# Inner products of the key projection one row block earlier, and a pair's first two key features inside its query projection

## The chip, the cores and the metric

The kernel runs on one core of a Trainium2 chip. The metric is the device time of one launch in microseconds (us). The kernel before took 1494.13 us, the median of 3 runs (1493.5 to 1495.38).

## What is computed

A layer norm of x (1250 rows, 1024 columns) feeds two branches: a two-layer graph convolution, and a linear attention with 16 heads of 64 columns and 256 random features. Their sum with x goes through a second layer norm and a mixture of 8 experts with the best 2 taken per row. The change touches the attention alone:

```python
q = heads(hidden_states @ Wq)
k = heads(hidden_states @ Wk)
v = heads(hidden_states @ Wv)
q_prime = jax.nn.relu(q @ proj)
k_prime = jax.nn.relu(k @ proj)
kv = jnp.einsum('bhsf,bhsd->bhfd', k_prime, v)
attn = jnp.einsum('bhsf,bhfd->bhsd', q_prime, kv)
norm = jnp.einsum('bhsf,bhf->bhs', q_prime, k_prime.sum(axis=2))[..., None]
attn = attn / (norm + EPS)
```

## The kernel before

**Number format.** Every fp32 product is made of three passes over high and low parts (`COMBOS`): high by high, high by low, low by high. So each result that leaves PSUM and is multiplied again is read out twice: ScalarE (ACT) copies it into the high part, then VectorE (DVE) subtracts that copy from PSUM and writes the low part. Only after the second reading is the PSUM region free (an `AT` product is only copied out, by ACT, and its norm for h = 0 by DVE).

**Attention by pairs.** The 16 heads are worked as 8 pairs, p = 0 to 7. Rows come in 10 tiles of 125, and a projection has 1250 columns as three pieces of 418. A pair is this work on TensorE (PE):

- `("K", p)` and `("Q", p)`: key and query projection (`slab_product`, L1829), 8 row blocks kt = 0 to 7 of 9 matmuls each.
- `("KK", p, i)`, i = 0 to 9: key features of row tile i (L1936), 4 matmuls; the ReLU is in the read-out (ACT L1052, DVE L1421). PSUM has three banks for them.
- `("KV", p, i)`: kv sum over the tiles (L1951), 6 matmuls, into its own bank `kvb`. `("S", p)` is its transpose (L1761).
- `("QP", p, h, f)`: query features of head h, half f (`feature_product`, L1771), 6 matmuls; read out by ACT L1064 and DVE L1438.
- `("AT", p, h)`: attention product of head h (`attention_product`, L1785), 18 matmuls, which needs `S` and both `QP` of its head.
- `RC` on DVE: the reciprocal of the norm (L1452) and the product with it (L1170, `num`). `RH` splits the result (`att_h`, `att_l`), and it is stored to `at_d`.
- `E`: a group of edges of the adjacency matrix, 4 bf16 matmuls (L1663) from one-hot tiles that DVE makes (`EO`, L1174); ACT copies the sum to `stage`, and GpSimd adds it to memory by DMA.

**Work inside work.** A pair's `QP(p,0,1)`, `AT(p,0)`, `QP(p,1,0)` and `QP(p,1,1)` don't stand alone on PE: they are issued between row blocks of the next key projection `K(p+1)`, `AT(p,1)` behind block 1 of `Q(p+1)`, and the groups `E` of edges behind blocks 2, 4, 5, 6 and 7 of `K(p+1)` (`PARTS`) and block 5 of `Q(p+1)`. In `K(p+1)` the order within one kt is: row block, then group, then transpose (kt = 0), then `AT` or `QP`. In the kernel before these lie at:

```python
if kt == 0:
    kv_transposes(p)
if kt == 3:
    attention_product(("AT", p, 0))
feature = {1: ("QP", p, 0, 1), 4: ("QP", p, 1, 0), 6: ("QP", p, 1, 1)}.get(kt)
```

**PSUM.** Two regions of three banks, slot 0 and slot 1, take nearly all products; `lsb` and `kvb` are single banks. `places_of()` walks `ORDER`: an ordinary product takes the region whose turn it is, and a product listed in `INNER` takes the other one. `free_slot(k)` makes PE wait until the product that had the region before `k` (`BEFORE[k]`) has been read out. For pair p from 1 to 6 this gives: `QP(p,0,0)`, `QP(p,0,1)`, `AT(p,0)`, `QP(p,1,0)`, `QP(p,1,1)` and then `Q(p+1)` follow one another in slot 0, each waiting for the one before; `K(p+1)`, then `AT(p,1)`, then the key features `KK(p+1, ...)` follow one another in slot 1.

**Order of the engines.** The list `ORDER` from `steps()` is the order in which every engine takes its own part of each step, and the semaphore counts come from positions in it. ACT and DVE work strictly in that order. Around the change, DVE's order in `K(p+1)` is `EO`, low part of a slab (`P`), `S`, `EO`, `QP(p,0,1)`, `EO`, `VL` (low part of the values), `AT(p,0)`, `EO`, `QP(p,1,0)`, `EO`, `QP(p,1,1)`, `K(p+1)`, `P`, `EO`, `EO`, `RC(p)`, then `KK(p+1,0)`, `KK(p+1,1)` and `KK(p+1,2)`. ACT's has `QP(p,0,1)`, `E`, `VL`, `AT(p,0)`, `E`, `QP(p,1,0)`, `E`, `QP(p,1,1)`, `E`, `K(p+1)`.

**The last pair** has no next projection to hide in. Its steps run one behind the other (p = 7), and two things are bound to DMA there: `AT(7,0)` is read out into tiles that the stores of pair 6 must have left (`att_stored`), and SyncE (SP) has begun to load the stored pairs back for the output projection, the first three of them when `Q(7)` is complete (`load_att`, L675). GpSimd's queue writes two blank tiles of 1680 KB in the same stretch, behind the last group of edges.

Of the kernel before, what the change touches and what calls it, by code (L numbers as in the profile page):

```python
# [28 lines left out]
T = 125  # L29
# [3 lines left out]
KD = D // 128  # L33
# [73 lines left out]
def steps():  # L107
# [30 lines left out]
    o += [("EO", q0[1]), ("VL", 0), ("P", 2)] + [("EO", g) for g in q0[2:]] + [("E", g) for g in q0] + [("Q", 0)]  # L138
    for p in range(PAIRS):
        more = p + 1 < PAIRS  # L140
        o += [("KK", p, 0), ("KK", p, 1), ("KK", p, 2)]
        if p:
            last = WITHIN[("Q", p)][1]
            o += [("EP", last), ("E", last)]
        for i in range(3, NT):
            o += [("KV", p, i - 3), ("KK", p, i)] + {4: [("QE", p, 0)], 7: [("QE", p, 1)]}.get(i, [])
        if not more:
            o += [("KV", p, NT - 3), ("KV", p, NT - 2), ("RH", p - 1), ("QP", p, 0, 0), ("KV", p, NT - 1), ("KC", p),
                  ("QP", p, 0, 1), ("S", p)]
            o += [("QP", p, 1, 0), ("QP", p, 1, 1), ("AT", p, 0), ("AT", p, 1), ("RC", p), ("RH", p)]  # L150
            continue
        o += [("KV", p, NT - 3)] + ([("RH", p - 1)] if p else [])
        o += [("QP", p, 0, 0), ("KV", p, NT - 2), ("KV", p, NT - 1), ("KC", p)]
        g, (q0, q1) = WITHIN[("K", p + 1)], WITHIN[("Q", p + 1)]
        n = SLAB[("K", p + 1)] + 1
        o += [("EO", g[0]), ("P", n), ("S", p), ("EO", g[1]), ("QP", p, 0, 1), ("E", g[0]), ("EO", g[2]), ("VL", p + 1),
              ("AT", p, 0), ("E", g[1]), ("EO", g[3]), ("QP", p, 1, 0), ("E", g[2]), ("EO", g[4]), ("QP", p, 1, 1),
              ("E", g[3]), ("K", p + 1), ("E", g[4])]
        o += [("P", n + 1)] if n + 1 < len(SLABS) else []
        o += [("EO", q0), ("AT", p, 1), ("EO", q1), ("E", q0), ("Q", p + 1), ("RC", p)]  # L160
    for f in range(KD):
        if f == KD - 1:
            o += [("DT",), ("ZP", 1, 0)]
# [47 lines left out]
ORDER = steps()  # L211
INNER = {("XT", i) for i in range(1, NT)} | {("AT", p, 1) for p in range(PAIRS - 1)}
INNER |= {("FT", i) for i in range(NT - 1)}
INNER |= {k for p in range(PAIRS - 1) for k in (("S", p), ("QP", p, 0, 1), ("AT", p, 0), ("QP", p, 1, 0), ("QP", p, 1, 1))}
OTHER = INNER | {("QP", p, 0, 0) for p in range(PAIRS - 1)}
AMID = {(6, 3): ("RT", 0), (7, 3): ("PX", 0), (8, 1): ("RT", 1), (8, 6): ("PX", 1)}
# [17 lines left out]
def places_of():  # L234

    place, before, last, turn = {}, {}, {}, 0
    for k in ORDER:
        if k[0] not in PSUM_KINDS:
            continue
        if k[0] == "KK":  # L240
            place[k] = turn
            before[k] = last.get(turn) if k[2] == 0 else before[("KK", k[1], 0)] if k[2] < 3 else ("KK", k[1], k[2] - 3)
            last[turn] = k
            continue
        if k[0] == "OT" or k in OTHER:
            place[k] = 1 - turn
        elif k[0] in ("R", "RT"):
            place[k] = 2 + (k[0] == "RT")
        elif k[0] == "PX":
            place[k] = 3  # L250
        else:
            place[k] = turn
            turn = 1 - turn
        before[k] = last.get(place[k])
        last[place[k]] = k
    return place, before
# [43 lines left out]
def build(nc, x, src_cols, dst_cols, dst_groups, slabs, wv, w1, w2, wr, proj, feat_rows, consts, turns, tie,  # L300
          iota, keys, eye, pe, blank, before, list_blank, tokens, expert_at, b2_rows, out):
    ctx = ExitStack()
    with ctx:
# [298 lines left out]
        def kk_bank(k):  # L602

            return slot[SLOT[k]][:T, 512 * (k[2] % 3):512 * (k[2] % 3) + 2 * FEAT]
# [1028 lines left out]
        def _(ten):  # L1633
# [120 lines left out]
            def kv_transposes(p):  # L1754
# [6 lines left out]
                    mm = ten.transpose(lsb[:, 128 * q:128 * q + 128], kvt[:, 128 * q:128 * q + 128], ident[:, :])  # L1761
                mm.then_inc(s_full, 1)

            def feature_product(k, ps):

                p, h, f = k[1:]
                if h == 0 and f == 0:
                    ten.wait_ge(dve_done, DVED[("QE", p, 0)])
                for c, part in enumerate((proj_h, proj_l[h])):
                    for q in range(3):  # L1770
                        mm = ten.matmul(ps[:, 512 * q:512 * q + CW], part[:, 128 * f:128 * f + 128],  # L1771
                                        q_s[h][:, CW * q:CW * q + CW], start=(c == 0), stop=(c == 1))
                mm.then_inc(psum_full, 1)
# [40 lines left out]
            def slab_product(k, ps):  # L1814
# [5 lines left out]
                for kt in range(KD):  # L1820
                    if k == ("O", 0) and kt < KD - 1:
                        ten.wait_ge(at_landed[kt], 32)
                    if k == ("O", 0) and kt == KD - 1:
                        ten.wait_ge(dve_done, DVED[("RH", PAIRS - 1)])
                    if k == ("H", 1, 0) and kt == KD - 1:
                        ten.wait_ge(dve_done, DVED[("Z", 1, KD - 1)])
                    for c, (a, b) in enumerate(COMBOS):
                        for q in range(3):
                            mm = ten.matmul(ps[:, 512 * q:512 * q + CW], w[a][:, kt, :],  # L1829
                                            big[b][:, kt, CW * q:CW * q + CW],  # L1830
                                            start=(kt == 0 and c == 0), stop=(kt == KD - 1 and c == 2))
                    if kt == 2 and k[0] == "O" and k[1]:
                        mix_transposes(k[1] - 1)
                    if kt == 1 and k[0] == "Q" and k[1]:
                        attention_product(("AT", k[1] - 1, 1))
                    if kt == KD - 1:
                        mm.then_inc(psum_full, 1)
                    for g, part in zip(inside, PARTS[len(inside)]):
                        if part == kt:
                            if k[0] == "K" and k[1] and g == inside[0]:  # L1840
                                ten.wait_ge(dve_done, DVED[("S", k[1] - 1)])
                            group_product(g)
                    if k[0] == "K" and k[1]:
                        p = k[1] - 1
                        if kt == 0:
                            kv_transposes(p)
                        if kt == 3:
                            attention_product(("AT", p, 0))
                        feature = {1: ("QP", p, 0, 1), 4: ("QP", p, 1, 0), 6: ("QP", p, 1, 1)}.get(kt)
                        if feature:  # L1850
                            free_slot(feature)
                            feature_product(feature, sums[SLOT[feature]])

            for k in ORDER:
# [74 lines left out]
                elif kind == "KK":  # L1929

                    p, i = k[1], k[2]
                    if i == 0:
                        ten.wait_ge(dve_done, DVED[("K", p)])
                    for h in range(2):
                        for c, part in enumerate((proj_h, proj_l[h])):
                            mm = ten.matmul(kk_bank(k)[:, FEAT * h:FEAT * h + FEAT], k_s[h][:, T * i:T * i + T], part[:, :],  # L1936
                                            start=(h == 0 and c == 0), stop=(c == 1), skip_group_check=True)
                elif kind == "KV":


# [215 lines left out]
```

## Time and profile before

| | us |
|---|---|
| median of 3 runs | 1494.13 |
| the profiled execution | 1493.13 |
| its span, first to last instruction | 1491.5 |
| PE busy | 1415.6 (95%) |
| DVE busy | 852.9 (57%) |
| ACT busy | 535.4 (36%) |

The profile is of one execution. Its engine rows name the source line, the operation and the tiles (out<-in). PE matmuls are pipelined: a matmul's time reaches into the next one's, so distances between two starts are what a step costs. A row with x3 is three matmuls, and its start is that of the first. "[0.68 <-DVE qp_l L1438]" means that the engine had sat idle for 0.68 us and that the wait was ended by that work of DVE. The pairs of heads fill the stretch from about 178 to 604 us, and pairs 1 to 7 repeat with a period of 56.2 us.

### The profile page before, as it was taken

How to read it: one execution, taken by the hardware profiler on the slowest of the kernel's cores; microseconds unless marked ns; L12 is line 12 of the kernel's file. 1: busy time of each engine (PE TensorE's matmuls, PEld its weight loads, DVE VectorE, ACT ScalarE, POOL GpSimd, SP SyncE). 2: the span in 40 equal slices, each digit the busy share in tenths (PEclk: the TensorE clock that was granted, in tenths of full speed). 3: DMA queues.
4: the chain of work that ended last, by engine and by line, in shares of the span. 5: the costliest groups of instructions: out<-in, count | busy, mean ns of one | idle time of the engine just before them, and what ended most of it. 6: DMA issues, size and time to landing. Idle time of an engine off the chain costs nothing.

```text
span 1491.5 us, 20042 instructions
## 1 busy us (share of the span) xinstructions
PE 1415.6 (95%) x7718; PEld 1308.4 (88%) x7718; DVE 852.9 (57%) x1563; ACT 535.4 (36%) x621; POOL 184.9 (12%) x182
## 2 busy tenths in 40 slices
PE   6999899999999999999999999999999759999995
PEld 5788899999999998899999999999788658888884
DVE  7564678778778778622766233354667734433340
ACT  4333254354354354232122133322112235444441
POOL 0012210100110111000000000000001442223311
PEclk9999999999999999999999999999999869999998
DMA  9765433243233336686342033221565587877863
GB/s 310 237 157 122 78 52 78 46 83 74 50 80 74 54 80 214 229 199 166 97 125 70 29 98 103 81 77 46 165 177 146 176 218 188 221 205 181 199 151 77
DMA packets 97187, 194.34 MB, mean 130 GB/s; under 512 B 31715, under 2 KB 62426, under 8 KB 95373
## 3 DMA queue, kind: packets, MB, share of 16 engines
q1 hardware_dynamic: 76324, 145.83, 33.3%
q0 software_dynamic: 20768, 47.22, 17.4%
q8 instruction: 62, 1.02, 0.3%
q14 instruction: 33, 0.27, 0.1%
HBM read 129.78 MB, written 73.13 MB: 136 GB/s over the span
## 4 chain that ended last, share of the span: by engine, by line
PE 72%; DMA 14%; DVE 6%; ACT 3%; issue 2%; SPq 1%; POOL 0%; POOLq 0%; ACTq 0%; DVEq 0%
PE slot L1829 24%; PE slot L1911 12%; DMA adj_d<-stage 8%; PE slot L2057 7%; PE slot L2025 6%; PE slot L1987 5%; PE slot L1785 3%; PE kvb L2057 3%; PE kvb L1951 3%; PE slot L1771 2%; DMA adj_d<-eye_dram 2%; PE slot L2040 2%; DMA mix_d<-mixn 1%; PE slot L1936 1%; DMA dx<-x_dram 1%
## 5 line engine op out<-in xcount | busy, mean ns | idle before, releaser
L1829 PE MATMUL slot<-big_hi,slab_h 128*128 128x418 f32 x768 | 194.7, 361 | 10.8 <-DVE qp_l L1438 4.8
L1829 PE MATMUL slot<-big_lo,slab_h 128*128 128x418 f32 x768 | 189.3, 355 | 0.0
L1829 PE MATMUL slot<-big_hi,slab_l 128*128 128x418 f32 x768 | 188.2, 353 | 0.0
L1829 PEld LDWEIGHTS slot<-big_hi,slab_h 128*128 128x128 f32 x768 | 140.4, 190 | 16.6 <-DVE qp_l L1438 6.4
L1829 PEld LDWEIGHTS slot<-big_hi,slab_l 128*128 128x128 f32 x768 | 145.2, 189 | 2.3
L1829 PEld LDWEIGHTS slot<-big_lo,slab_h 128*128 128x128 f32 x768 | 145.1, 189 | 2.2
L839 POOL DMA_DIRECT2D adj_d<-stage x80 | 66.7, 834 | 484.8 <-ACT stage L919 372.3
L1911 PE MATMUL slot<-adj,xs_h 125*128 125x418 f32 x480 | 118.2, 354 | 0.8 <-DVE ztmp L1170 0.5
L1911 PE MATMUL slot<-adj,xs_l 125*128 125x418 f32 x480 | 117.4, 352 | 0.0
L1174 DVE TENSOR_SCALAR oh_src<-lane,src_lo 125x125 bf16<-125x125 f16 x320 | 84.6, 265 | 25.7 <-PE kvb L1663 18.0
L864 POOL DMA_INDIRECT list_d<-rec,spots x20 | 27.9, 1397 | 529.7 <-issue 512.4
L1911 PEld LDWEIGHTS slot<-adj,xs_h 125*128 125x128 f32 x480 | 90.4, 189 | 2.2 <-DVE ztmp L1170 0.7
L1911 PEld LDWEIGHTS slot<-adj,xs_l 125*128 125x128 f32 x480 | 90.5, 189 | 1.2
L1174 DVE TENSOR_SCALAR oh_key<-key_iota,key_rel 125x240 bf16<-125x240 int16 x320 | 90.7, 283 | 0.0
L1170 DVE TENSOR_TENSOR ws_l<-ws_raw,ws_h 128x1024 fp32r<-128x1024 f32 x32 | 38.9, 1219 | 85.6 <-ACT ws_h L919 85.6
L1170 DVE TENSOR_TENSOR slab_l<-slab_raw,slab_h 128x1024 fp32r<-128x1024 f32 x34 | 41.6, 1223 | 57.8 <-ACT slab_h L919 57.6
L899 POOL DMA_INDIRECT out_dram<-y,lists x32 | 49.1, 1533 | 181.3 <-ACT y L919 175.6
L1452 DVE RECIPROCAL nrm<-nrm 128x1254 f32<-128x1254 f32 x8 | 63.9, 7993 | 9.6 <-ACT nrm L919 9.6
L2057 PE MATMUL slot<-xe_h,ws_h 128*128 128x420 f32 x176 | 64.6, 367 | 2.2 <-DVE xe_l L1170 2.2
L1421 DVE SCALAR_TENSOR_TENSOR kk_l<-slot,kk_h 125x512 fp32r<-125x512 f32 x80 | 51.6, 686 | 26.0 <-ACT kk_h L1052 25.5
L1052 ACT ACTIVATE kk_h<-slot 125x512 fp32r<-125x512 f32 x80 | 46.0, 597 | 50.8 <-PE slot L1936 50.4
L2057 PE MATMUL slot<-xe_l,ws_h 128*128 128x420 f32 x176 | 63.2, 359 | 0.0
(316 smaller groups left out, 2940.9 us busy)
## 6 DMA issues: line engine op xcount, KB each, us to landing
slab_raw<-slabs_dram SPq DMA_DIRECT2D x40, 512.0 KB, 4.2
ws_raw<-w_dram SPq DMA_DIRECT2D x36, 512.0 KB, 7.3
adj_d<-stage POOLq DMA_DIRECT2D x81, 117.2 KB, 3.1
w_raw<-w_dram SPq DMA_DIRECT2D x9, 1024.0 KB
adj_d<-eye_dram POOLq DMA_DIRECT2D x1, 6250.0 KB, 24.8
raw<-adj_d SPq DMA_DIRECT2D x3, 1828.8 KB
dx<-x_dram SPq DMA_DIRECT2D x10, 448.0 KB
xn_d<-dx SPq DMA_DIRECT2D x10, 448.0 KB
```

The source lines that it names most:

```text
L839: pool.dma_start(adj_d[:, bass.ds(first, SPAN), :].rearrange("p d j -> p (d j)"), stage[g % 3][:, :], accum_op=ALU.add).then_inc(e_added, 16)
L899: pool.indirect_dma_start(out, bass.IndirectOffsetOnAxis(ap=lists[:, e, i, 0:1].bitcast(U32), axis=0), y[i][:, :], None, compute_op=ALU.ad ...
L1052: act.activation(kk_p[k[2] % 3][0][:, :], kk_bank(k), ACT.Relu).then_inc(act_done, 1)
L1170: return dve.tensor_tensor(o, a, b, op)
L1174: dve.tensor_scalar(o, a, s1, None, op0)
L1421: dve.scalar_tensor_tensor(out=kk_p[k[2] % 3][1][:, :], in0=kk_bank(k), scalar=0.0, in1=kk_p[k[2] % 3][0][:, :].bitcast(F32), op0=ALU.max, ...
L1452: link(dve.reciprocal(nrm[:, :], nrm[:, :]))
L1829: mm = ten.matmul(ps[:, 512 * q:512 * q + CW], w[a][:, kt, :], big[b][:, kt, CW * q:CW * q + CW], start=(kt == 0 and c == 0), stop=(kt == ...
L1911: mm = ten.matmul(ps[:, 512 * q:512 * q + CW], xs_p[t % 2][a][:, j, :], adj[:, j, CW * q:CW * q + CW], start=(j == 0 and a == 0), stop=(j ...
L1987: mm = ten.matmul(ps[:T, 512 * q:512 * q + 512], big[b][:, kt, T * i:T * i + T], rows_p[kt][a][:, 512 * q:512 * q + 512], start=(kt == 0 a ...
L2025: mm = ten.matmul(to[:RT_, 512 * q:512 * q + 512], a_p[a][:, f, RT_ * i:RT_ * i + RT_], w2_p[e % 2][b][:, f, 512 * q:512 * q + 512], start ...
L2057: mm = ten.matmul(ps, w[a][:, kt, :], xe[b][:, kt, :], start=(kt == 0 and c == 0), stop=(kt == KD - 1 and c == 2))
```

## The change

Three of the four inner products in `K(p+1)` are issued one row block earlier: `QP(p,0,1)` behind block 0 and not 1, `AT(p,0)` behind 2 and not 3, `QP(p,1,1)` behind 5 and not 6. `QP(p,1,0)` stays behind block 4. For pairs 1 to 7, `KK(p,0)` and `KK(p,1)` are issued inside `Q(p)`, behind its row blocks 5 and 6, and not behind it; `KK(p,2)` and the rest stay. They become `INNER`, so that they keep the slot that they had (1), and on every engine's list they stand behind `RC(p-1)`, as they did, and ahead of `Q(p)`. No instruction is added or removed.

```diff
@@ steps()
-        o += [("KK", p, 0), ("KK", p, 1), ("KK", p, 2)]
+        o += [] if p else [("KK", p, 0), ("KK", p, 1)]
+        o.append(("KK", p, 2))
...
-        o += [("EO", q0), ("AT", p, 1), ("EO", q1), ("E", q0), ("Q", p + 1), ("RC", p)]
+        o += [("EO", q0), ("AT", p, 1), ("EO", q1), ("E", q0), ("RC", p), ("KK", p + 1, 0),
+              ("KK", p + 1, 1), ("Q", p + 1)]
@@
+INNER |= {("KK", p, i) for p in range(1, PAIRS) for i in range(2)}
@@ places_of()
-            place[k] = turn
-            before[k] = last.get(turn) if k[2] == 0 else before[("KK", k[1], 0)] if k[2] < 3 else ("KK", k[1], k[2] - 3)
-            last[turn] = k
+            place[k] = 1 - turn if k in INNER else turn
+            before[k] = (last.get(place[k]) if k[2] == 0 else before[("KK", k[1], 0)] if k[2] < 3
+                         else ("KK", k[1], k[2] - 3))
+            last[place[k]] = k
@@ TensorE
+            def key_features(k):
+
+                p, i = k[1:]
+                if i == 0:
+                    ten.wait_ge(dve_done, DVED[("K", p)])
+                for h in range(2):
+                    for c, part in enumerate((proj_h, proj_l[h])):
+                        mm = ten.matmul(kk_bank(k)[:, FEAT * h:FEAT * h + FEAT], k_s[h][:, T * i:T * i + T], part[:, :],
+                                        start=(h == 0 and c == 0), stop=(c == 1), skip_group_check=True)
+                mm.then_inc(psum_full, 1)
@@ slab_product(k, ps)
                     if kt == 1 and k[0] == "Q" and k[1]:
                         attention_product(("AT", k[1] - 1, 1))
+                    if k[0] == "Q" and k[1] and KD - 3 <= kt < KD - 1:
+                        free_slot(("KK", k[1], kt - KD + 3))
+                        key_features(("KK", k[1], kt - KD + 3))
@@
-                        if kt == 3:
+                        if kt == 2:
                             attention_product(("AT", p, 0))
-                        feature = {1: ("QP", p, 0, 1), 4: ("QP", p, 1, 0), 6: ("QP", p, 1, 1)}.get(kt)
+                        feature = {0: ("QP", p, 0, 1), 4: ("QP", p, 1, 0), 5: ("QP", p, 1, 1)}.get(kt)
```

The walk of `ORDER` on TensorE calls `key_features(k)` for the other key features, in place of the same loop written there.

## Rows read from the trace of the kernel before

**Rows 1.** Stretches: length, busy (count) of PE, PEld, DVE, ACT, POOL, PEclk, DMA, GB/s.

```profile
175.00:197.00 22.00, 18.01 (x125) 17.52 (x126) 11.97 (x27) 9.91 (x16) 3.31 (x4) 0.92 0.29 44
253.00:309.00 56.00, 54.83 (x336) 53.25 (x335) 44.83 (x83) 26.67 (x34) 5.80 (x7) 1.00 0.35 69
```

**Rows 2.** Waits of PE in 175 to 606 us: total, times, longest.

```profile
PE kvb L1951 <- DVE kk_l L1421: 6.4, 10, 2.7
PE slot L1829 <- DVE qp_l L1438: 4.8, 7, 0.7
```

**Rows 3.** Timeline of PE (start, length), K(2): block 1, group, block 3, AT(1,0).

```profile
255.00 0.82 PE L1829 MATMUL slot<-big_hi,slab_h 128*128 128x418 f32 x3
...
259.68 0.57 PE L1663 MATMUL lsb<-oh_key,oh_src 125*125 125x240 bf16 x4
260.02 0.82 PE L1829 MATMUL slot<-big_hi,slab_h 128*128 128x418 f32 x3
...
261.83 0.73 PE L1785 MATMUL slot<-qp_h,s_h 128*128 128x418 f32 x3
```

**Rows 4.** Timeline of DVE, same stretch: QP(1,0,0), first one-hot, QP(1,0,1).

```profile
252.99 1.46 DVE L1438 SCALAR_TENSOR_TENSOR qp_l<-slot,qp_h 128x1254 fp32r<-128x1254 f32 x1
254.36 0.25 DVE L1174 TENSOR_SCALAR oh_src<-lane,src_lo 125x125 bf16<-125x125 f16 x1
...
259.41 1.46 DVE L1438 SCALAR_TENSOR_TENSOR qp_l<-slot,qp_h 128x1254 fp32r<-128x1254 f32 x1 [0.40 <-ACT qp_h L1064]
```

**Rows 5.** Timeline of PE, rear of K(2): QP(1,1,0), QP(1,1,1), last group, Q(2).

```profile
267.35 0.82 PE L1771 MATMUL slot<-qT,proj_h 128*128 128x418 f32 x3
...
272.76 0.82 PE L1771 MATMUL slot<-qT,proj_h 128*128 128x418 f32 x3
...
275.70 0.57 PE L1663 MATMUL lsb<-oh_key,oh_src 125*125 125x240 bf16 x4
276.96 0.84 PE L1829 MATMUL slot<-big_hi,slab_h 128*128 128x418 f32 x3 [0.68 <-DVE qp_l L1438]
```

**Rows 6.** Timeline of ACT, same stretch: QP(1,1,1), then both copies of K(2).

```profile
274.19 1.22 ACT L1064 ACTIVATE qp_h<-slot 128x1254 fp32r<-128x1254 f32 x1 [2.92 <-PE slot L1771]
...
275.90 2.45 ACT L919 ACTIVATE kT<-slot 64x1254 fp32r<-64x1254 f32 x2 [0.24 <-PE slot L1829]
```

**Rows 7.** Timeline of DVE, same stretch: QP(1,1,1), then both low parts of K(2).

```profile
275.44 1.46 DVE L1438 SCALAR_TENSOR_TENSOR qp_l<-slot,qp_h 128x1254 fp32r<-128x1254 f32 x1 [2.52 <-ACT qp_h L1064]
277.14 2.94 DVE L1170 TENSOR_TENSOR kT<-slot,kT 64x1254 fp32r<-64x1254 f32 x2 [0.24 <-ACT kT L919]
```

**Rows 8.** Timeline of PE: AT(1,1); key features, group, KV(2,0); KV(2,5).

```profile
280.51 0.73 PE L1785 MATMUL slot<-qp_h,s_h 128*128 128x418 f32 x3
...
294.65 0.28 PE L1936 MATMUL slot<-proj_h,kT 128*125 128x256 f32 x1
...
296.07 0.57 PE L1663 MATMUL lsb<-oh_key,oh_src 125*125 125x240 bf16 x4
296.70 0.39 PE L1951 MATMUL kvb<-kk_h,v_h 125*128 125x256 f32 x1
...
303.34 0.39 PE L1951 MATMUL kvb<-kk_h,v_h 125*128 125x256 f32 x1 [0.43 <-DVE kk_l L1421]
```

**Rows 9.** Timeline of DVE: end of RC(1), key features 0 to 2 of pair 2.

```profile
293.42 1.47 DVE L1170 TENSOR_TENSOR num<-num,nrm 128x1254 f32<-128x1254 f32 x1
295.95 1.89 DVE L1421 SCALAR_TENSOR_TENSOR kk_l<-slot,kk_h 125x512 fp32r<-125x512 f32 x3 [1.07 <-ACT kk_h L1052]
```

**Rows 10.** Timeline of SP, last pair: first load at the end of Q(7), store.

```profile
575.98 0.33 SPq L675 DMA_DIRECT2D big_hi<-at_d  x1
...
590.79 2.38 SPq L756 DMA_DIRECT2D at_d<-att_l  x1
```

**Rows 11.** Timeline of ACT, last pair: AT(7,0), released by the store.

```profile
604.25 1.21 ACT L919 ACTIVATE num<-slot 64x1254 f32<-64x1254 f32 x1 [6.58 <-DMA at_d<-att_l]
```

**Rows 12.** Timeline of PE: first block of the output projection.

```profile
605.81 0.81 PE L1829 MATMUL slot<-big_hi,slab_h 128*128 128x418 f32 x3 [1.32 <-ACT num L919]
```

More of the change, by code:

```diff
@@ L1931, in _ @@
                     p, i = k[1], k[2]
[L1932 to L1937, printed above, removed]
+                    key_features(k)
+                    continue
                 elif kind == "KV":
```

## The prediction

> **What bounds the kernel now.** I read the stretches first: in one period of a pair (253 to 309 us) PE is busy for 54.83 of 56 us at the full granted clock, DVE for 44.83 and ACT for 26.67 [rows 1]. So PE sets the pace, and since the change neither adds nor removes an instruction, it can move the time only through what PE waits for. The list of PE's waits comes next: the read-out of query features ends 7 waits with 4.8 us in all, the read-out of key features 10 waits with 6.4 us, of which 2.7 us in one, in pair 0, which the change leaves alone [rows 2]. Then I walked one period on the timelines, engine by engine, to see where PE stands against the time at which it could have gone on. The reader is to see three places there.
>
> *At the start of Q(2).* QP(1,1,1) starts at 272.76 and Q(2) at 276.96 [rows 5]. Q(2) takes the slot that QP(1,1,1) had, so it waits for ACT (274.19 to 275.41) and DVE (275.44 to 276.90), which follow each other without a gap [rows 6, 7]. From start of the product to the release of its slot that is **4.20 us**. Unhindered, Q(2) would follow the last group, which begins at 275.70 and takes 0.34 us (259.68 to 260.02 for another group), so at 276.04 [rows 3, 5]. PE loses **0.92 us**.
>
> *At KV(2,0).* The group ahead of it starts at 296.07, so KV could start at 296.41; it starts at 296.70, when key feature 0 has been read out [rows 8]. **0.29 us** lost. The page hides this one, as the group's modelled end covers it.
>
> *At KV(2,5)*: idle for 0.43 us [rows 8], the read-out of a key feature stands behind that of the query projection. Nothing in the change moves these three against each other, and I leave it at nothing.
>
> **The front of K(p+1): QP(p,0,1) and AT(p,0) earlier.** What lies between 255.00 and the group at 259.68 is the same work in another order, and the group still ends at 260.02, so AT(1,0) could start at 260.02, where block 3 stands today, and not at 261.83 [rows 3]. It needs the slot of QP(1,0,1), and so DVE. QP(1,0,1) itself can start at 255.00: the slot of QP(1,0,0) is released when DVE ends at 254.45 [rows 3, 4]. But DVE then has one-hots, slab, transpose and again one-hots in front of QP(1,0,1), from 254.36 without a gap; today it waits for only 0.40 us between them and the read-out at 259.41 [rows 4]. So the read-out of a product that comes 1.8 us earlier can move forward by only 0.40 us, or 0.48, as DVE's next instruction starts 0.09 us before the end of the one ahead (254.36 against 252.99 + 1.46) [rows 4]. I take 0.48: 258.93 + 1.46 = 260.39, and PE follows 0.06 us later (276.90 to 276.96) [rows 5, 7], at 260.45. A **new wait of 0.43 us** (0.51 at the other bound). The one who waits is PE with everything behind it.
>
> **The rear of K(p+1): QP(p,1,1) earlier.** Its position moves from behind block 6 to behind block 5, and QP(1,1,0) stays, at 267.35 [rows 5], now 0.43 later. Between the two there is left one product, one block and one group, the same work as between QP(1,1,1) and Q(2) today: 275.70 - 272.76 + 0.34 = 3.28 us [rows 3, 5]. But QP(1,1,1) needs the slot that QP(1,1,0) had, 4.20 us after its start by the chain above. A **new wait of 0.92 us**: it is the very wait that is taken away from Q(2), at another place. In exchange Q(2) finds its slot free: block 6, group, block 7 and group now lie between. **0.92 us removed.**
>
> **What that does to AT(p,1).** It is not in the diff, but it takes the slot of K(p+1). ACT starts to copy K(2) at 275.90 and DVE ends at 277.14 + 2.94 = 280.08 [rows 6, 7]; with 0.06 to PE that is 4.24 us after the copy begins. Today AT(1,1) starts 4.61 us after it, at 280.51 [rows 6, 8], and part of that distance is the wait at Q(2). With this gone the distance is 4.61 - 0.92 = 3.69 us, and PE waits for **0.55 us**. The copies can't begin earlier, K(2) is complete only just before the last group, and ACT is idle ahead of them (0.24 us) [rows 6].
>
> **The key features inside Q(p).** KK(p,0) and KK(p,1) need slot 1 after AT(p-1,1): four row blocks lie between, and ACT's two copies of K took 2.45 us [rows 6], so no wait. They cost PE what they did: three of them fill 294.65 to 296.07, 0.47 us each [rows 8]; a change of neighbour moves the time of three matmuls by up to 0.09 us (0.82 behind a group, 0.73 elsewhere [rows 3]), so between -0.09 and +0.09 us I take nothing. DVE stands in RC until 293.42 + 1.47 = 294.89 and idles for 1.07 us before the three low parts from 295.95, 1.89 us [rows 9]. With all that is ahead 1.0 us later, RC ends at about 295.9 and the low part of KK(2,0) at 296.6, while KV(2,0) is due at about 297.4: the **0.29 us is removed**, and RC in front of the key features on DVE costs nothing, with 0.8 us to spare.
>
> **The sum for a pair.** Removed: 0.92 + 0.29 = 1.21 us. New: 0.43 + 0.92 + 0.55 = 1.90 us. Net +0.69 us, and seven transitions (K(1) to K(7)) make **+4.8 us**. I take K(1) as equal to the others.
>
> **The last pair.** There PE is not the bound. AT(7,0) is copied out at 604.25, after 6.58 us of waiting for a store of pair 6 that SP began at 590.79 [rows 10, 11], and the output projection stood still for 1.32 us behind that copy [rows 12]. The store shares the DMA engines with loads that SP issues from the end of Q(7) on, at 575.98 [rows 10], and with GpSimd's blank tiles. The change brings the end of Q(7) nearer to the store: KV(7,0) comes 296.70 - 294.65 = 2.05 us after the end of Q now [rows 8], and then one key feature and one group after it, 0.47 + 0.34, so 1.24 us of distance are gone. If the DMA engines are the limit all the way from the end of Q(7), these 1.24 us are paid in full, if the store's own time counts, not at all. The blank tiles start with the last group, which comes nearer too. Between 0 and 1.2 I take the middle, **+0.6 us**.
>
> Together +5.4 us. The profiled execution took 1493.13 us, of which 1491.5 are the span; it is 1.0 us under the median of 1494.13, so I add to either: about 1498.5 us in an execution like the profiled one, and **1499.5 us** as the median.
>
> **The rivals.** *The moved waits fall under other work* (faster). Then only the removed ones count, 7 x 1.21 = 8.5 us, 1485.7 us. For it speaks that the waits in question are real and regular, seven of each. Against it that the slot's release is a chain of ACT and DVE without slack in it [rows 6, 7]; it could come true only if QP(1,1,1) did not need the slot of QP(1,1,0). *The wait only changes its place* (no difference). If AT(p,1) finds its slot free after all, the sum of a pair is 1.21 against 1.35, 7 x 0.14 = 1.0 us, with the last pair 1495.7. It decides at 0.37 us: so much slack AT(1,1) has today (280.51 against 280.08 + 0.06) [rows 7, 8]. *The clock gives way under more waits* (slower still). In 175 to 197 us, with the wait of 2.7 us in it [rows 2], the granted clock has a mean of 0.92 [rows 1]: 0.08 x 22 / 0.5 = 3.5 us at 1.2 GHz instead of 2.4, or 1.8 us lost. Once for a pair that is 12 us more, 1512 us. Against it: the period with waits of 0.68 and 0.43 us in it shows 1.00 [rows 1, 5, 8], and the new ones are under 1 us. The Trainium skill (TensorE: Matmul & The Clock Gate, A second HAM failure mode: psum-queue depth-cycling) speaks for this rival: TensorE that is idle for a moment between groups of matmuls, cycling through PSUM banks, may see its clock fall and rise again. By that rule this rival would be likely; the trace doesn't show it in the pairs. *The change doesn't do what it says*: the same instructions in a different order can't be left out, and I give it no chance of its own.
>
> **How the numbers follow.** My forecast gets 0.80; its own range is 1497.2 to 1501.5 (a pair at 0.69 - 0.25 or + 0.2, which is the bounds above, 0.08 and 0.09, and about as much again for what modelled ends hide; the last pair at 0 or 1.2). No difference gets 0.10, the faster rival 0.08, the clock 0.02. The range 1495.0 to 1502.5 holds the first and the larger part of the second. A difference of 0.2%, 3.0 us, is about what a measurement of this kernel can tell from none; the lower part of my own range is near to it, so slower by more gets 0.78, within it 0.14, faster 0.08.
>
> **What the profile after would show.** PE idle ahead of QP(p,1,1) (L1771) and AT (L1785) seven times each, released by DVE's `qp_l`, and ahead of AT(p,1) released by `kT`; no wait of L1829 for `qp_l` at Q, and no gap before KV(p,0). The period of a pair grows from 56.2 to about 56.9 us. I am wrong if AT(p,1) doesn't wait for `kT`, if DVE's `qp_l` of QP(p,0,1) comes more than 0.5 us earlier against the start of K(p+1), or if the period gets shorter.

## The result

The changed kernel takes 1500.82 us (median of 5 runs, 1500.29 to 1501.87) against 1494.13 us: 6.7 us, or 0.45%, **slower** (ratio 1.0045, 95% interval 1.0033 to 1.0056). Run again on another occasion, on one chip with the last two experiments, it gave 1.0042 (1.0029 to 1.0055). The profiled execution took 1501.87 us, with a span of 1500.2; it is the slowest of the five, so spans differ by more (8.7 us) than medians do; a table in the part on the prediction says where. In the experiments a difference in us is worked out from the ratio, and the ratio compares with the kernel before as it ran on the same occasion (medians of 1493.1 to 1494.9 us). The medians themselves can lie up to 2 us further apart.

TensorE's waits over the pairs, as in [rows 2] (engine, line and tile, who ended the wait: total us, times, longest). Lines have moved: L1844 is the row block of a projection, L1786 an inner product of the features, L1800 the attention product, L1775 the key features, L1965 the kv sum.

```profile
PE kvb L1965 <- DVE kk_l L1425: 6.5, 10, 2.7
PE slot L1786 <- DVE qp_l L1442: 5.6, 9, 0.7
PE slot L1800 <- DVE kT L1174: 2.8, 7, 0.4
PE slot L1800 <- DVE qp_l L1442: 1.9, 7, 0.3
```

The reader is to see that the seven waits of a projection for `qp_l` [rows 2] have gone, and that waits at three other places have come. Seven of the nine at L1786 are those of QP(p,1,1); two, of 0.36 and 0.46 us, belong to the last pair, as before. Seven waits of AT(p,1) are for `kT`, and seven of AT(p,0) are for `qp_l`. The timeline of PE in K(2) and Q(2) (start, length of the merged matmuls) answers [rows 3, 5, 8]:

```profile
259.77 0.57 PE L1667 MATMUL lsb<-oh_key,oh_src 125*125 125x240 bf16 x4
260.64 0.82 PE L1800 MATMUL slot<-qp_h,s_h 128*128 128x418 f32 x3 [0.29 <-DVE qp_l L1442]
...
267.93 0.82 PE L1786 MATMUL slot<-qT,proj_h 128*128 128x418 f32 x3
...
272.13 0.84 PE L1786 MATMUL slot<-qT,proj_h 128*128 128x418 f32 x3 [0.69 <-DVE qp_l L1442]
...
277.55 0.82 PE L1844 MATMUL slot<-big_hi,slab_h 128*128 128x418 f32 x3
...
281.65 0.83 PE L1800 MATMUL slot<-qp_h,s_h 128*128 128x418 f32 x3 [0.41 <-DVE kT L1174]
...
297.35 0.57 PE L1667 MATMUL lsb<-oh_key,oh_src 125*125 125x240 bf16 x4
297.69 0.37 PE L1965 MATMUL kvb<-kk_h,v_h 125*128 125x256 f32 x1
...
304.31 0.39 PE L1965 MATMUL kvb<-kk_h,v_h 125*128 125x256 f32 x1 [0.43 <-DVE kk_l L1425]
```

| wait in front of | before | forecast | after, from the rows |
|---|---|---|---|
| AT(p,0) | 0 | 0.43 | 260.64 - (259.77 + 0.34) = 0.53 |
| QP(p,1,1) | 0 | 0.92 | 272.13 - (267.93 + 3.28) = 0.92 |
| Q(p+1) | 0.92 | 0 | 0, it starts at 277.55 without a wait |
| AT(p,1) | 0 | 0.55 | 281.65 - (277.55 + 3.53) = 0.57 |
| KV(p+1,0) | 0.29 | 0 | 297.69 - (297.35 + 0.34) = 0 |
| sum | 1.21 | 1.90 | 2.02 |

Here 3.28 us is one inner product, one block and one group [rows 3, 5], and 3.53 us lies between the starts of Q(2) and AT(1,1) when nothing waits: 3.55 by [rows 5, 8], less 0.02 that a start out of a wait costs there. From KV(2,5) at 304.31 to the same place of pair 7, at 589.66, are 285.35 us, a period of 57.07; before, from 303.34 [rows 8] to 584.47, it was 56.23. Seven times 0.84 us are 5.9 us.

The last pair, as in [rows 10 to 12]: SP's queue, then ACT, then PE.

```profile
582.43 0.33 SPq L679 DMA_DIRECT2D big_hi<-at_d  x1
...
595.98 2.34 SPq L760 DMA_DIRECT2D at_d<-att_l  x1
```

```profile
611.34 1.21 ACT L923 ACTIVATE num<-slot 64x1254 f32<-64x1254 f32 x1 [8.48 <-DMA at_d<-att_l]
...
613.80 1.21 ACT L923 ACTIVATE num<-slot 64x1254 f32<-64x1254 f32 x1
```

```profile
612.90 1.39 PE L1844 MATMUL slot<-big_hi,slab_h 128*128 128x418 f32 x3 [3.22 <-ACT num L923]
```

The output projection waits 3.22 us for the copy of AT(7,0), and not 1.32. The store of pair 6 landed 15.26 us after it was issued, 13.36 before.

### The profile page after: what moved, and what is told of

Its sections match the earlier page's. It is cut to its first block, busy times and chain, and to the rows that moved or that the text cites. A ratio compares the mean times of both kernels' runs of the same rounds, so it can differ in the third digit from the quotient of the medians.

```text
span 1500.2 us, 20042 instructions
## 1 busy us (share of the span) xinstructions
PE 1418.2 (95%) x7718; PEld 1310.1 (87%) x7718; DVE 853.8 (57%) x1563; ACT 537.1 (36%) x621; POOL 184.9 (12%) x182
## 4 chain that ended last, share of the span: by engine, by line
PE 67%; DMA 14%; DVE 11%; ACT 4%; issue 2%; SPq 1%; POOL 0%; POOLq 0%; ACTq 0%; DVEq 0%
PE slot L1844 20%; PE slot L1929 12%; DMA adj_d<-stage 8%; PE slot L2071 7%; PE slot L2039 6%; PE slot L2001 5%; PE slot L1800 3%; PE kvb L2071 3%; DVE qp_l L1442 2%; PE kvb L1965 2%; PE slot L1775 2%; DMA adj_d<-eye_dram 2%; PE slot L2054 1%; DMA mix_d<-mixn 1%; DVE kT L1174 1%
## 5 line engine op out<-in xcount | busy, mean ns | idle before, releaser
L1844 PE MATMUL slot<-big_hi,slab_h 128*128 128x418 f32 x768 | 194.0, 361 | 7.8 <-ACT num L923 3.2
L1844 PE MATMUL slot<-big_lo,slab_h 128*128 128x418 f32 x768 | 190.2, 356 | 0.0
L1844 PE MATMUL slot<-big_hi,slab_l 128*128 128x418 f32 x768 | 189.1, 354 | 0.0
L1844 PEld LDWEIGHTS slot<-big_hi,slab_h 128*128 128x128 f32 x768 | 141.9, 191 | 11.4 <-ACT num L923 3.5
L1844 PEld LDWEIGHTS slot<-big_hi,slab_l 128*128 128x128 f32 x768 | 146.2, 190 | 2.4
L1844 PEld LDWEIGHTS slot<-big_lo,slab_h 128*128 128x128 f32 x768 | 145.9, 190 | 2.0
L868 POOL DMA_INDIRECT list_d<-rec,spots x20 | 27.9, 1397 | 530.3 <-issue 512.9
```

## The experiments

Theory: a PSUM slot is released 4.20 us after the start of an inner product, DVE works in the order of its list, and RC starts with AT(p,1); so each product that is moved nearer to the one ahead of it in its slot takes the wait with it, and the products behind it, which had lived on that wait, begin to wait too. The last pair is bound by DMA from the end of Q(7) on. Rival: the key features inside the query projection are what costs, and the longer store is chance.

**The inner products alone** (the kernel before, with the three new places).

```diff
-                        if kt == 3:
+                        if kt == 2:
                             attention_product(("AT", p, 0))
-                        feature = {1: ("QP", p, 0, 1), 4: ("QP", p, 1, 0), 6: ("QP", p, 1, 1)}.get(kt)
+                        feature = {0: ("QP", p, 0, 1), 4: ("QP", p, 1, 0), 5: ("QP", p, 1, 1)}.get(kt)
```

> The inner products of the key projection one row block earlier, alone; the key features stay behind the query projection, as before. Theory (waits for PSUM slots only move, and one more appears): per transition the new waits at AT(p,0), QP(p,1,1) and AT(p,1) measured in the changed kernel, 0.53 + 0.92 + 0.57 us, against 0.92 us removed at Q, net +1.10 us, seven times: 7.7 us slower than before (7 to 8.5), and the store of pair 6 in the last pair lands 13 to 14 us after its issue, as before. Rival (the key features inside the query projection are what costs, by breaking up its stream of matmuls): under 4 us slower than before.

Measured: 1503.41 us, ratio 1.0047 (1.0031 to 1.0064), 7.0 us slower; the medians are 8.5 us apart. Its waits in 195 to 575 us, which hold the key projections of pairs 1 to 7, and so seven of each:

```profile
PE slot L1771 <- DVE qp_l L1438: 4.8, 7, 0.7
PE slot L1785 <- DVE kT L1170: 2.8, 7, 0.4
...
PE slot L1785 <- DVE qp_l L1438: 2.0, 7, 0.3
```

All three new waits are there without the key features. From KV(2,5) at 299.81 to KV(7,5) at 586.64 the period is 57.37 us, 1.14 above the kernel before; 1.10 was expected. So the loss is of the inner products, and the rival is out.

**The key features alone** (the changed kernel, with the inner products back at blocks 1, 3, 4 and 6).

```diff
-                        if kt == 2:
+                        if kt == 3:
                             attention_product(("AT", p, 0))
-                        feature = {0: ("QP", p, 0, 1), 4: ("QP", p, 1, 0), 5: ("QP", p, 1, 1)}.get(kt)
+                        feature = {1: ("QP", p, 0, 1), 4: ("QP", p, 1, 0), 6: ("QP", p, 1, 1)}.get(kt)
```

> The first two key features of pairs 1 to 7 inside the query projection, alone; the inner products stay where they were. Theory: 0.29 us less in front of KV(p,0), seven times 2.0 us less up to the last pair, and there 1.2 to 1.9 us given back at the store, which then takes about 15 us to land instead of 13.4: in all between -0.9 and 0 us against before. Rival (key features inside cost something of their own): slower than before by over 1 us, and the period of a pair not shorter than 56.24 us.

Measured: ratio 0.9994 (0.9980 to 1.0008), no difference that can be told. The period is read from two rows of PE's timeline five pairs apart, the first matmuls of KV(2,5) and KV(7,5):

```profile
306.38 0.39 PE L1965 MATMUL kvb<-kk_h,v_h 125*128 125x256 f32 x1 [0.43 <-DVE kk_l L1425]
```

```profile
586.07 0.39 PE L1965 MATMUL kvb<-kk_h,v_h 125*128 125x256 f32 x1 [0.43 <-DVE kk_l L1425]
```

(586.07 - 306.38) / 5 = 55.94 us, 0.29 less than before: the gain in the pairs is the wait that was removed, and a key feature between two blocks costs nothing of its own that the period shows. Over seven pairs that is 2.0 us; the runs don't show them.

**The key features inside, but not in pair 7** (the kernel with the key features alone). The edit leaves `("KK", 7, 0)` and `("KK", 7, 1)` behind `Q(7)`; of its diff one place is shown, and `steps()` and `INNER` are changed to match.

```diff
-                    if k[0] == "Q" and k[1] and KD - 3 <= kt < KD - 1:
+                    if k[0] == "Q" and 0 < k[1] < PAIRS - 1 and KD - 3 <= kt < KD - 1:
```

> As the run with the key features alone, but pair 7 keeps its first two behind its query projection, so that the distance from the end of Q(7) to the store of pair 6 is as before. Theory (the last pair is bound by DMA from the end of Q(7) on): six times 0.29 us less, 1.7 us faster than before, the store lands 13.4 us after its issue, and this kernel is 0.8 to 1.7 us faster than the one with the key features inside Q(7) as well. Rival (the longer store was chance): the store takes the same time in both, and this kernel is 0.3 us slower than that one.

Measured: ratio 0.9993 (0.9980 to 1.0005), the same as with pair 7. The store took 14.32 us and not 13.4, so neither theory's number came out, and the runs can't tell 1 us. What bears on it is the distance of the first load of the last pair from the landing of the store, in all the profiles that still have the blank tiles there:

| kernel | first load | store issued | landed after | load to landing |
|---|---|---|---|---|
| before | 575.98 | 590.79 | 13.36 | 28.2 |
| inner products alone | 578.15 | 592.95 | 13.52 | 28.3 |
| last product alone | 578.25 | 593.06 | 13.78 | 28.6 |
| attention later | 592.47 | 606.94 | 13.54 | 28.0 |
| keys, not pair 7 | 573.95 | 588.75 | 14.32 | 29.1 |
| changed | 582.43 | 595.98 | 15.26 | 28.8 |
| changed, again | 583.83 | 597.38 | 14.31 | 27.9 |
| keys alone | 578.84 | 592.38 | 15.20 | 28.7 |
| one-hots behind | 578.35 | 591.89 | 14.63 | 28.2 |

The upper five issue the store 14.5 to 14.8 us after the first load, the lower four 13.5 us after it. The last column has a mean of 28.4 us in both, with 0.4 us of scatter from profile to profile. So, over this range, the landing follows the end of Q(7) and not the issue of the store, and the 1.24 us by which the store came nearer are given back, as far as nine profiles with that scatter can tell.

**The last product alone** (the kernel before, QP(p,1,1) behind block 5).

```diff
-                        feature = {1: ("QP", p, 0, 1), 4: ("QP", p, 1, 0), 6: ("QP", p, 1, 1)}.get(kt)
+                        feature = {1: ("QP", p, 0, 1), 4: ("QP", p, 1, 0), 5: ("QP", p, 1, 1)}.get(kt)
```

> Only the last inner product, QP(p,1,1), from behind row block 6 to behind row block 5. Theory: a wait of 0.92 us in front of it, none in front of Q, and 0.57 us in front of AT(p,1) for the read-out of K: seven times 0.57, 4.0 us slower than before. Rival (the wait only changes its place, and AT(p,1) waits in the changed kernel because of the other two moves): within 0.5 us of before, and AT(p,1) does not wait.

Measured: 1499.60 us, ratio 1.0029 (1.0018 to 1.0040), 4.3 us slower.

```profile
PE slot L1771 <- DVE qp_l L1438: 4.8, 7, 0.7
PE slot L1785 <- DVE kT L1170: 2.8, 7, 0.4
```

4.8 us of waits in seven stand now at the inner product (L1771), the same sum as at the projection before [rows 2], and AT(p,1) waits for K's low part, without the other two moves. The period is (586.75 - 302.41) / 5 = 56.87 us, 0.64 more than before. This one edit is about two thirds of the loss.

**The attention product one block later** (the changed kernel with AT(p,1) behind block 2 of the query projection).

```diff
-                    if kt == 1 and k[0] == "Q" and k[1]:
+                    if kt == 2 and k[0] == "Q" and k[1]:
                         attention_product(("AT", k[1] - 1, 1))
```

> The changed kernel with AT(p,1) behind row block 2 of the query projection and not behind block 1. Theory (AT(p,1) waits for the read-out of K, and RC on DVE starts with AT(p,1)): no wait of AT(p,1) for kT, 0.57 us less, but AT(p,1) then starts 1.15 us later than in the changed kernel, RC ends as much later, and KV(p,0) waits about 0.9 us for key feature 0, which it did not in the changed kernel: 0.3 to 0.4 us more per transition, 2 to 3 us slower than the changed kernel, 9 to 10 us slower than before. Rival (the wait at AT(p,1) comes from something else, as the S of its pair): the wait stays after the move.

Measured: 1504.61 us, ratio 1.0061 (1.0043 to 1.0080), 9.1 us slower than before.

```profile
PE kvb L1965 <- DVE kk_l L1425: 7.2, 13, 0.7
PE slot L1786 <- DVE qp_l L1442: 4.8, 7, 0.7
PE slot L1800 <- DVE qp_l L1442: 1.9, 7, 0.3
```

No wait for `kT` is left, and the kv sum waits 13 times and not 6 in 195 to 575 us. Six are new, of 0.69 us each, at KV(p,0) behind RC (a seventh, of pair 7, comes at 594.00); the seventh of the others is that of pair 0, which lies inside the window here. The period is 57.36 us, from 256.50 to 600.64 in six, 0.29 more than in the changed kernel. So AT(p,1) is held between the read-out of K ahead of it and the reciprocal behind it, and moving it one block does not win.

**DVE's one-hots behind the read-out** (the changed kernel, one entry of the order).

```diff
-        o += [("EO", g[0]), ("P", n), ("S", p), ("EO", g[1]), ("QP", p, 0, 1), ("E", g[0]), ("EO", g[2]), ("VL", p + 1),
+        o += [("EO", g[0]), ("P", n), ("S", p), ("QP", p, 0, 1), ("EO", g[1]), ("E", g[0]), ("EO", g[2]), ("VL", p + 1),
```

> The changed kernel with DVE's second set of one-hots behind its read-out of QP(p,0,1) and not ahead of it. Theory (the wait of AT(p,0) is DVE's queue): the read-out starts when ACT is done, 1.3 us earlier, AT(p,0) does not wait, and each transition is 0.53 us shorter: 3.7 us faster than the changed kernel, 3 us slower than before. The one-hots are then made 1.4 us later, far ahead of their group. Rival (AT(p,0) waits for the transpose S or for ACT): no difference to the changed kernel.

Measured: 1497.04 us, ratio 1.0015 (1.0001 to 1.0029), 2.2 us slower than before.

```profile
PE slot L1786 <- DVE qp_l L1442: 4.8, 7, 0.7
PE slot L1800 <- DVE kT L1174: 2.8, 7, 0.4
PE kvb L1965 <- DVE kk_l L1425: 2.6, 6, 0.4
```

The wait of AT(p,0) for `qp_l` is gone and the other two are untouched. The period is (585.58 - 302.74) / 5 = 56.57 us, 0.50 less than in the changed kernel. The wait came from what stood ahead in DVE's order.

**The blank tiles early** (the changed kernel; GpSimd writes them in pairs 3 and 4).

```diff
+                if g == WITHIN[("K", 4)][0]:
+                    pool.dma_start(flat_d[N:N + CAP, :], blank).then_inc(blanks_in, 16)
+                if g == WITHIN[("K", 5)][0]:
+                    pool.dma_start(out[N:N + CAP, :], blank).then_inc(blanks_in, 16)
                 first = pool.value_load(base_i[0:1, g:g + 1], min_val=0, max_val=N - 1)
...
-            pool.dma_start(flat_d[N:N + CAP, :], blank).then_inc(blanks_in, 16)
-            pool.dma_start(out[N:N + CAP, :], blank).then_inc(blanks_in, 16)
```

> The changed kernel with GpSimd's two blank tiles (3.4 MB) written during pairs 3 and 4, where the DMA engines are a third busy, and not in the last pair. Theory (the store of pair 6 shares the DMA engines with loads and blank tiles): it lands 5 to 8 us after its issue instead of 15, AT(7,0) is copied out without a wait, and the first block of the output projection starts about 3 us sooner: 2.5 to 3.5 us faster than the changed kernel. Rival (the store waits for something else, as its turn on SP's queue): it still takes over 12 us.

Measured: 1498.60 us, ratio 1.0035 (1.0021 to 1.0048) against before; the changed kernel's was 1.0045, and the intervals overlap, so the runs alone don't show a gain. The trace shows it more sharply. The store was issued at 594.87 and landed 5.5 us later, and not 15.26, as the theory had it (5 to 8 us); the rival, its turn on SP's queue, is out. ACT copied AT(7,0) out as soon as PE had made it:

```profile
605.19 1.21 ACT L925 ACTIVATE num<-slot 64x1254 f32<-64x1254 f32 x1 [3.42 <-PE slot L1802]
...
609.88 1.22 ACT L925 ACTIVATE num<-slot 64x1254 f32<-64x1254 f32 x1
```

From KV(7,5) at 588.57 that is 16.6 us; in the changed kernel it was 611.34 - 589.66 = 21.7, before 604.25 - 584.47 = 19.8 [rows 11]. The last copy, of AT(7,1), has to wait for PE then. It ends the chain that RC starts from, and comes 609.88 - 588.57 = 21.3 us after KV(7,5), where it was 613.80 - 589.66 = 24.1 in the changed kernel and 614.26 - 591.07 = 23.2 in its second profile: 1.9 to 2.8 us less.

**The best order** puts the lessons together: a distance of two blocks between QP(p,1,0) and QP(p,1,1), the one-hots and the values' parts behind the read-outs that PE waits for, and the edge group of the query projection ahead of AT(p,1), with its one-hots in DVE's idle time before K's low part. The blank tiles are early too, by the edit of the experiment before, which is not printed again.

```diff
-        o += [("EO", g[0]), ("P", n), ("S", p), ("EO", g[1]), ("QP", p, 0, 1), ("E", g[0]), ("EO", g[2]), ("VL", p + 1),
-              ("AT", p, 0), ("E", g[1]), ("EO", g[3]), ("QP", p, 1, 0), ("E", g[2]), ("EO", g[4]), ("QP", p, 1, 1),
-              ("E", g[3]), ("K", p + 1), ("E", g[4])]
+        o += [("EO", g[0]), ("P", n), ("S", p), ("QP", p, 0, 1), ("EO", g[1]), ("E", g[0]), ("EO", g[2]), ("AT", p, 0),
+              ("VL", p + 1), ("QP", p, 1, 0), ("E", g[1]), ("EO", g[3]), ("E", g[2]), ("EO", g[4]), ("QP", p, 1, 1),
+              ("E", g[3]), ("EO", q0), ("K", p + 1), ("E", g[4])]
         o += [("P", n + 1)] if n + 1 < len(SLABS) else []
-        o += [("EO", q0), ("AT", p, 1), ("EO", q1), ("E", q0), ("RC", p), ("KK", p + 1, 0),
-              ("KK", p + 1, 1), ("Q", p + 1)]
+        o += [("E", q0), ("AT", p, 1), ("EO", q1)]
+        o += [("RC", p), ("KK", p + 1, 0), ("KK", p + 1, 1), ("Q", p + 1)]
...
                     if kt == 1 and k[0] == "Q" and k[1]:
+                        group_product(inside[0])
                         attention_product(("AT", k[1] - 1, 1))
...
-                        if part == kt:
+                        if part == kt and not (k[0] == "Q" and k[1]):
...
-                        feature = {0: ("QP", p, 0, 1), 4: ("QP", p, 1, 0), 5: ("QP", p, 1, 1)}.get(kt)
+                        feature = {0: ("QP", p, 0, 1), 3: ("QP", p, 1, 0), 5: ("QP", p, 1, 1)}.get(kt)
```

> A version meant to leave out the waits that the theory names: on top of the changed kernel, one-hots behind the read-out of QP(p,0,1), the values' parts behind AT(p,0), QP(p,1,0) behind row block 3 (so that two blocks lie between it and QP(p,1,1)), the group of edges of the query projection ahead of AT(p,1) with its one-hots made before the read-out of K, and the blank tiles early. Theory: no wait for QP(p,1,1) and AT(p,0), about 0.3 us at AT(p,1), none at Q and KV(p,0): a period of about 55.3 us instead of 56.2, 6 to 7 us less over the pairs and 2 to 3 us less in the last one, 8 to 10 us faster than before. Rival: a further queue shows up, and the period stays above 56 us.

Measured: 1485.26 us, ratio 0.9937 (0.9917 to 0.9957), 9.4 us faster than before.

```profile
PE kvb L1968 <- DVE kk_l L1427: 2.6, 6, 0.4
```

This is the whole list for 195 to 575 us: of all the waits that the theory named, the one at KV(p,5) alone is left. The 0.3 us that were expected at AT(p,1) are not there either. The edits were made together, and what each is worth here was not run. The period is (577.45 - 300.57) / 5 = 55.38 us. Once more, beside the next one:

> The version with the best order once more, beside its successor and beside the changed kernel on the same chip: 8 to 10 us faster than before, period 55.4 us.

It gave 1484.80 us, 0.9945 (0.9932 to 0.9958), 8.2 us faster than before, and the same period, (578.39 - 301.57) / 5 = 55.36 us.

**The query's read-out ahead of key feature 2**, against that last wait.

```diff
-        o.append(("KK", p, 2))
+        o += [("QE", p, 0), ("KK", p, 2)] if p else [("KK", p, 2)]
...
-            o += [("KV", p, i - 3), ("KK", p, i)] + {4: [("QE", p, 0)], 7: [("QE", p, 1)]}.get(i, [])
+            o += [("KV", p, i - 3), ("KK", p, i)] + {4: [] if p else [("QE", p, 0)], 7: [("QE", p, 1)]}.get(i, [])
```

> The version with the best order so far, and in it the read-out of the query projection's first head, QE(p,0), moved from behind key feature 4 to ahead of key feature 2, for pairs 1 to 7. Theory (PE stops for 0.43 us at KV(p,5), 0.59 us against the time at which it could start, as QE stands between two key features on ACT and DVE; with key features 0 and 1 read out early, QE fits ahead of feature 2): the wait at KV(p,5) goes, one of about 0.3 us comes at KV(p,2), and the period falls by 0.3 to 0.4 us to about 55.0 us: 2 to 3 us faster than the version without. Rival (ACT and DVE are full there, so that the wait only changes its place): the period stays at 55.4 us.

Measured: 1488.74 us, 0.9969 (0.9958 to 0.9980): 4.6 us faster than before, and 3.6 us slower than the version without it.

```profile
PE slot L1788 <- DVE qT L1176: 2.0, 6, 0.3
PE kvb L1968 <- DVE kk_l L1427: 1.5, 6, 0.3
```

The wait at KV(p,5) has gone and that at KV(p,2) has come, as expected. What was not expected is a third one, of 0.34 us: QP(p,0,0) now waits for the read-out of the query's second head (`qT`). It stands behind key feature 7, and the wait at KV(p,5) may have given it the time; that is argued from the order and was not tested. The period is (576.90 - 298.08) / 5 = 55.76 us, 0.38 more, so both of the outcomes that were expected, a shorter period and the same one, failed. Of the 3.6 us this explains 2.7. Another 0.5 lie in the last pair, where the kv sum waits once for 1.06 us (584.87) and not 0.35: from SP's first load to the copy of AT(7,1) are 602.47 - 573.42 = 29.05 us, and 598.75 - 570.22 = 28.53 without the edit. The rest is open.

**The changed kernel again.**

> The changed kernel once more, on the same chip as the two best versions: 5.5 to 7.5 us slower than before, period 57.1 us; the store of pair 6 lands 15 us after its issue if its lengthening is the change's and not chance.

Ratio 1.0042 (1.0029 to 1.0055), 6.3 us, period (591.07 - 305.73) / 5 = 57.07 us. Its store took 14.31 us and not 15, with the same 28 us from the first load. The 15 us that were expected of the change didn't come again, but the landing, 27.9 us after the first load, is in the spread of the table.

## Why the prediction was right

**Direction, size and mechanism held.** 1499.5 us was forecast and 1500.82 measured, +5.4 against +6.7 us. Step by step:

- *PE is the bound and only its waits count*: right for the pairs. PE's busy time hardly moved (1415.6 to 1418.2 us, and 1415.3 in the second profile), and the periods follow the waits in every experiment.
- *Removed, 0.92 at Q and 0.29 at KV(p,0)*: both right to 0.02 us, the second shown by the key features alone (period 0.29 us shorter).
- *QP(p,1,1) takes its wait along*: right, 0.92 us. The last product alone shows it.
- *AT(p,1) waits for K's read-out*: right, 0.57 for 0.55 us. This term decides the sign. Without it, by the forecast's own sizes, the change would have given 0.14 us per pair away and nothing to measure; with the last product alone it cost 4.3 us.
- *AT(p,0) waits for DVE's queue*: right in its mechanism (the one-hots behind the read-out remove it), too small in size, 0.53 for 0.43 us; in K(3) it is 0.48. DVE started the read-out where forecast (259.04, 0.73 us ahead of the group, for 0.75). PE followed it after 0.14 us where I had taken 0.06 from the other waits. I have no row that says why.
- *The last pair*: right in its mechanism, and the middle of 0 and 1.2 us was the wrong choice. The nine distances from first load to landing speak for the upper bound, 1.24 us.
- *K(1) like the others*: right. From KV(0,5) to KV(1,5) it is 247.25 - 190.20 = 57.05 us, and 247.15 - 190.89 = 56.26 before, 0.79 more beside 0.84 in the other pairs.
- *A key feature between two blocks at nothing, and RC in front of the key features at nothing*: right. The key features alone show the first, and the low part of KK(2,0) ends 0.83 us before KV(2,0) starts, for 0.8 forecast.
- *The clock at nothing*: right in the pairs, not behind them (below). What it cost there was no term of the sum.

With the measured sizes the sum is 7 x 0.84 + 1.24 = 7.1 us, for 6.7 measured (4.9 to 8.4). The two under-sized terms are the difference: 7 x 0.15, of which 0.10 is AT(p,0) and the rest what a start out of a wait costs, and 0.6 us in the last pair.

No large errors had to cancel for this: both err the same way. Where the time went in the two profiled executions, against the one before (us):

| stretch | before | changed | changed, again |
|---|---|---|---|
| start to KV(0,5) | 190.89 | 190.20 | 191.64 |
| KV(0,5) to KV(7,5) | 393.58 | 399.46 | 399.43 |
| KV(7,5) to the copy of AT(7,1) | 22.25 | 24.14 | 23.19 |
| on to PE's restart behind its wait for DVE's `mixn` | 61.37 | 63.40 | 61.84 |
| the rest of the span | 823.4 | 823.0 | 822.9 |

The pairs give 5.9 us in both. The last pair gives 1.9 and 0.9, which scatter about 1.24. The first and the last row are scatter between executions, of up to 0.8 us. The fourth row has a cause of its own, which is the third rival's.

**The rivals.** That the moved waits fall under other work is refuted by the timeline. That the wait only changes its place is half true, for QP(p,1,1) against Q, and fails at AT(p,1). That the clock gives way is refuted in the pairs, and not behind them. In the pairs the granted clock is 1.00, as here, and so it is from 196 to 606 us as a whole (columns as in [rows 1]):

```profile
253.00:309.00 56.00, 54.18 (x329) 52.37 (x328) 44.08 (x83) 25.95 (x35) 5.80 (x7) 1.00 0.35 69
```

The clock that falls and rises again under short idle times, in the Trainium skill (TensorE: Matmul & The Clock Gate, A second HAM failure mode: psum-queue depth-cycling), is not borne out there, at waits under 1 us. At the end of the last pair it is different. These are the stretches of the wait of 3.22 us, and of what follows it:

```profile
609.00:612.00 3.00, 0.68 (x4) 0.32 (x2) 0.67 (x1) 0.66 (x1) 0.00 (x0) 1.00 1.00 368
612.00:619.00 7.00, 6.10 (x18) 5.86 (x19) 5.99 (x2) 2.96 (x3) 0.00 (x0) 0.51 1.01 414
619.00:622.00 3.00, 3.00 (x18) 2.97 (x17) 2.97 (x2) 0.00 (x0) 0.00 (x0) 1.00 0.79 326
```

Behind the wait the granted clock is down at its lower level, 1.2 GHz of 2.4, until about 619: the first two row blocks of the output projection take 619.13 - 612.90 = 6.23 us, and 609.35 - 605.81 = 3.54 us before, where the wait is 1.32 us long and the clock stays at 1.00. In the second profile it follows a wait of 2.25 us:

```profile
614.00:618.00 4.00, 4.00 (x14) 3.84 (x13) 3.73 (x1) 1.45 (x2) 0.00 (x0) 0.57 1.03 417
```

Of all the profiles that start this projection with a wait, three of the five with 2.25 us or more have such a fall (3.22, 2.60 and 2.25 us; not 3.15 and 2.27 us), and none of the four with 1.72 us or less. So the longer wait of the last pair brings a second cost, in some executions. In the first profile it is about 2.7 us of TensorE's pace, of which 2.0 us are left in the fourth row of the table; the second profile has 0.5 us there, which other profiles have without a fall (61.4 to 62.7 us in all). That is part of why the profiled execution was the slowest of the five. What it adds to the median is open: of the other executions only the mean clock is known.

## What to carry to other kernels

When products are interleaved by hand and share a PSUM slot, write down for each slot the chain of its users with the time from the start of a product to the release of its slot, and place each user at least so far behind the one before; moving only one of them moves the wait, and whoever had lived on that wait pays next. An idle stretch of the bounding engine is slack for every read-out queued at that time: before removing it, go through the next products of both slots and of each engine's queue. And check at the end of a repeated stage whether a transfer, and not the engine, sets the time from a fixed event on: there, work that comes nearer to that event gains nothing. Read the granted clock behind a long wait in short stretches, and of more than one profile: a mean over the kernel (0.979 here, 0.982 in the second profile and before) doesn't say where it fell.

## What the hardware showed beyond that

- Leaving a wait costs TensorE a little more than the idle time: at the kv sum the second matmul follows the first after 0.22 us instead of 0.12, so the 0.59 us that PE waits at KV(p,5) are 0.69 in its pace.
- The wait of AT(p,0) ends 0.14 us after the end of DVE's instruction, while those of QP(p,1,1) and AT(p,1) end 0.06 and 0.05 us after it, with the same kind of semaphore. It is so in all seven pairs, in both profiles of the changed kernel and with the inner products alone (0.14 to 0.15 us). The cause is open.
- Where two writes of 1680 KB stand is worth 1.9 to 2.8 us in the last pair's trace: in pairs 3 and 4 they leave the period at 57.07 us, (588.57 - 303.20) / 5, and in the last pair they hold up a store that TensorE waits for, which lands 15.3 or 14.3 us after its issue and not 5.5.
- A fall of the granted clock to 1.2 GHz behind a wait of a few us is not the change's alone: the kernel before has one too, behind its wait of 1.99 us for `mixn` at 668.09 (0.57 from 668 to 672 us, and 1.00 on both sides of it).
